# Self-attention scores of a perceiver layer: products of 128 rows by 256 columns, or four row groups of 32 rows by 64 columns over four PSUM banks

## What is computed

```
x = x + cross_attention(layernorm(x), ctx)       # 16 heads of 64, causal, softmax, w_o
x = x + self_attention(layernorm(x))             # 16 heads of 16
x = x + fp4_ffn(layernorm(x))                    # blockwise FP4 rounding of x, h and weights; silu(gate) * up; down
```

```
q, k, v = x @ Wq, x @ Wk, x @ Wv
scores  = q_h @ k_h.T                            # 32 x 32, upper triangle masked to -inf
out_h   = softmax(scores / 16) @ v_h
y       = concat(out_h) @ Wo + bo
```

## Time and profile before

| | us |
|---|---|
| executions | 588.86, 585.85, 585.41 |
| median | 585.85 |
| profiled execution | 588.76 |
| its span, first to last instruction | 586.8 |
| mean granted TensorE clock, share of full speed | 0.968 |

### The profile page before, as it was taken

How to read it: one execution, slowest core, us unless ns; L and a number is a source line. 1 busy time by engine, 2 the same in 40 slices (tenths; PEclk the granted TensorE clock), 3 DMA queues, 4 the chain that set the end, 5 groups by cost and what they waited for, 6 DMA issues and landing times.

```text
span 586.8 us, 18922 instructions
## 1 busy us (share of the span) xinstructions
PE 538.1 (92%) x7926; PEld 429.3 (73%) x7942; DVE 445.3 (76%) x866; ACT 234.2 (40%) x477; POOL 45.6 (8%) x84
## 2 busy tenths in 40 slices
PE   4979999999999999999965989999999999999865
PEld 3768888889888888988743756777777777777543
DVE  3627789888888888888940469988888888888852
ACT  1322233323233332323233456555555555555211
POOL 5000100000000000000020011111111111111100
PEclk9979999999999999999996889999999999999987
DMA  8991210112211012221200000000000000000000
GB/s 255 345 275 72 72 72 25 47 72 72 72 72 72 8 63 72 72 72 73 74 2 4 3 1 2 9 9 9 9 9 9 9 9 9 9 9 10 10 9 19
DMA packets 13801, 31.03 MB, mean 53 GB/s; under 512 B 976, under 2 KB 10704, under 8 KB 11728
## 3 DMA queue, kind: packets, MB, share of 16 engines
q1 hardware_dynamic: 13776, 30.67, 15.7%
HBM read 28.57 MB, written 2.10 MB: 52 GB/s over the span
## 4 chain that ended last, share of the span: by engine, by line
PE 47%; issue 30%; DVE 14%; ACT 4%; POOL 3%; POOLq 0%; DVEq 0%; ACTq 0%
PE bank L378 10%; PE bank L400 10%; PE bank L369 9%; PE bank L425 8%; PE bank L416 3%; ACT x_oT L502 2%; DVE f_xn L1394 2%; POOL f_rstd L1087 2%; DVE f_h L1403 1%; PE bank L1200 1%; PE bank L1178 1%; DVE f_amax_x L1489 1%; DVE f_xn L1528 1%; ACT a_kblocks L1302 1%; PE bank L1154 1%
## 5 line engine op out<-in xcount | busy, mean ns | idle before, releaser
L378 PEld LDWEIGHTS bank<-x_xcT,xwk 128*128 128x128 f32 x512 | 61.3, 197 | 2.8 <-issue 1.1
L378 PE MATMUL bank<-x_xcT,xwk 128*128 128x128 f32 x512 | 61.7, 280 | 1.4 <-ACT x_xcT L485 1.4
L400 PE MATMUL bank<-xwv,x_xcT 128*128 128x512 f32 x128 | 60.8, 618 | 1.0
L369 PE MATMUL bank<-x_xcT,xwq 128*128 128x128 f32 x512 | 59.8, 275 | 0.0
L425 PE MATMUL bank<-xwo,x_oT 128*128 128x256 f32 x256 | 58.0, 380 | 0.8 <-ACT x_oT L502 0.8
L369 PEld LDWEIGHTS bank<-x_xcT,xwq 128*128 128x128 f32 x512 | 58.5, 192 | 0.0
L516 ACT COPY x_k_blocks<-bank 64x512 f32<-64x512 f32 x32 | 18.6, 582 | 87.2 <-PE bank L378 87.0
L425 PEld LDWEIGHTS bank<-xwo,x_oT 128*128 128x128 f32 x256 | 47.5, 190 | 7.2 <-issue 1.4
L1154 PE MATMUL bank<-wdT,f_hqT 128*128 128x256 f32 x192 | 47.6, 400 | 4.3 <-DVEq L1419 2.3
L1302 ACT ACTIVATE a_kblocks<-bank,head_rows 128x256 f32<-128x256 f32 x128 | 48.4, 499 | 0.0
L1178 PE MATMUL bank<-wgT,f_xqT 128*128 128x192 f32 (+1 forms) x128 | 42.3, 475 | 3.7 <-DVE f_out L1360 3.7
(11 more groups left out here) (150 smaller groups left out, 931.4 us busy)
## 6 DMA issues: line engine op xcount, KB each, us to landing
x_ctx_slab<-in_ctx_dram SPq DMA_DIRECT2D x16, 1028.0 KB, 4.7
out_dram<-f_out SPq DMA_DIRECT2D x16, 128.0 KB, 1.7
xall<-in_x_dram SPq DMA_DIRECT2D x1, 1280.0 KB, 16.5
x_first_keys<-in_ctx_dram SPq DMA_DIRECT2D x4, 320.0 KB, 12.5
xwk<-in_L_xattn_w_k_dram SPq DMA_DIRECT2D x1, 1024.0 KB, 5.1
xwq<-in_L_xattn_w_q_dram SPq DMA_DIRECT2D x1, 1024.0 KB, 7.1
xwv<-in_L_xattn_w_v_dram SPq DMA_DIRECT2D x1, 1024.0 KB, 10.2
xwo<-in_L_xattn_w_o_dram SPq DMA_DIRECT2D x1, 1024.0 KB, 12.7
```

The source lines that it names most:

```text
L369: last = nc.tensor.matmul(bank67[:, j // 4, (j % 4) * P:(j % 4 + 1) * P], xwq[:, k, j * P:(j + 1) * P], xcT[:, k, :], start=(k == 0), stop ...
L378: last = nc.tensor.matmul(bank[2 + j // 4][:, (j % 4) * P:(j % 4 + 1) * P], xwk[:, k, j * P:(j + 1) * P], xcT[:, KD + k, :], start=(k == 0 ...
L400: last = nc.tensor.matmul(bank45[:, half, :], xcT[:, KD + k, :], xwv[:, k, half * 512:(half + 1) * 512], start=(k == 0), stop=(k == KD - 1))
```

## The change

Scores are made by 32 small products in place of 8 large ones. The 128 rows of q.T and k.T are eight heads of 16; a row group of 32 rows is two heads. `copy_qk` writes k.T twice, once with the odd and once with the even heads zeroed (`odd_rows`). `scores` multiplies 32 rows by 64 moving columns at `tile_position=(32 r, 32 b)`, row group r into bank 4 + r. The mask is four bf16 products of 128 columns. `odd_rows` is one reduction on VectorE at the end of cross-attention.

Four banks for the scores displace the others: gate goes to banks 2 and 3, transposed `f_xq` and the down product share the free columns of bank 3, q and k go to bank 5, the transposed `f_hq` to banks 4 and 0, v to bank 1 (which `values` and `output` use too), up stays in 6 and 7. With that come new waits on PE: `scores` waits for `f_hidden_ready` and has its two old waits ahead of the mask; `turn_xq` waits for `f_out_ready` and `f_hidden_ready`, no longer for `a_v_ready`; `output` waits for `a_v_ready`; up and `project_qk` wait for `a_shifted`; `project_v` waits for `a_out_ready` in place of `f_hidden_ready`.

```diff
-                a_kb = psb("a_kblocks", [P, KD, BT, HT, SQ])
+                a_kb = psb("a_kblocks", [P, KD, BT, 2, SQ])
...
-                h_bank = (bank[2], bank[0][:, 2 * P:])
-                down_bank = bank45[:, 1, 2 * P:2 * P + D]
+                RG = P // 32
+                HW = KD * 2 * SQ
+                gate_bank, up_bank = bank234567[:, 0:2, :], bank67
+                h_bank = (bank45[:, 0, :], bank[0][:, 2 * P:])
+                qk_bank = bank45[:, 1, :]
+                xq_bank = down_bank = gate_bank[:, 1, 2 * P:2 * P + D]
+                v_bank = bank[1][:, 0:D]
...
-                    def scores(t):
-                        nc.tensor.matmul(bank[2][:], causal_rows[:].rearrange("p b q -> p (b q)"),
-                                         key_copies[:].rearrange("p h k -> p (h k)"), start=True, stop=False)
+                    def scores(t, consumed):
+                        if consumed is not None:
+                            pe.wait_ge(s_f_h, consumed)
                         pe.wait_ge(s_a_kb, t + 1)
                         pe.wait_ge(s_a_qc, t + 1)
+                        for r in range(RG):
+                            nc.tensor.matmul(bank234567[:, 2 + r, 0:HW], causal_rows[:].rearrange("p b q -> p (b q)"),
+                                             key_copies[:, 0:HW // SQ].rearrange("p h k -> p (h k)"),
+                                             start=True, stop=False)
                         for j in range(KD):
-                            for b in range(BT):
-                                last = nc.tensor.matmul(bank[2][b * SQ:(b + 1) * SQ, j * HT * SQ:(j + 1) * HT * SQ],
-                                                        a_qT[:, j, b * SQ:(b + 1) * SQ],
-                                                        a_kb[:, j, b].rearrange("p h k -> p (h k)"),
-                                                        start=False, stop=(j == KD - 1), tile_position=(0, b * SQ))
+                            for r in range(RG):
+                                rows = slice(r * 32, (r + 1) * 32)
+                                for b in range(BT):
+                                    last = nc.tensor.matmul(
+                                        bank234567[b * SQ:(b + 1) * SQ, 2 + r, j * 2 * SQ:(j + 1) * 2 * SQ],
+                                        a_qT[rows, j, b * SQ:(b + 1) * SQ],
+                                        a_kb[rows, j, b].rearrange("p h k -> p (h k)"),
+                                        start=False, stop=(j == KD - 1), tile_position=(r * 32, b * SQ))
                         last.then_inc(s_a_s, 1)
...
-                    def project_v(t, hidden):
-
-                        if hidden is not None:
-                            pe.wait_ge(s_f_h, hidden)
+                    def project_v(t, weighed):
+
+                        if weighed is not None:
+                            pe.wait_ge(s_a_oc, weighed)
                         for k in range(KD):
-                            last = nc.tensor.matmul(bank67[:, 1, D:2 * D], n_xnT[:, k, :], swv[:, k, :],
+                            last = nc.tensor.matmul(v_bank, n_xnT[:, k, :], swv[:, k, :],
                                                     start=(k == 0), stop=(k == KD - 1))
...
                         if attend:
-                            scores(t)
+                            scores(t, t - 2 if down else None)
                         if gate:
-                            turn_xq(t - 2, attend)
+                            turn_xq(t - 2, t - 2 if down else None)
                         if norm:
-                            output(t - 1)
+                            output(t - 1, t + 1 if attend else None)
...
-                        for h in range(HT):
+                        for i in range(2):
                             last = nc.scalar.activation(
-                                a_kb[:, :, :, h, :], bank[3][:, KD * P:].rearrange("p (j b k) -> p j b k", j=KD, b=BT),
-                                ACT.Copy, scale=head_rows[:, h:h + 1])
+                                a_kb[:, :, :, i, :], qk_bank[:, KD * P:].rearrange("p (j b k) -> p j b k", j=KD, b=BT),
+                                ACT.Copy, scale=odd_rows[:, i:i + 1])
```

More of the change, by code:

```diff
@@ L1156, in down_product, with turn_xq, gate_up @@
                         last.then_inc(s_f_d, 1)
[L1158 to L1161, removed]
+                    def turn_xq(t, added):
+                        if not (isinstance(t, int) and t == 0):
                             pe.wait_ge(s_f_h, t)
+                        if added is not None:
+                            pe.wait_ge(s_f_out, added)
                         pe.wait_ge(s_f_xq, t + 1)
                         for k in range(KD):
-                            last = nc.tensor.transpose(bank67[:, 1, k * P:(k + 1) * P], f_xq[:, k * P:(k + 1) * P],
+                            last = nc.tensor.transpose(xq_bank[:, k * P:(k + 1) * P], f_xq[:, k * P:(k + 1) * P],
                                                        ident[:])
                         last.then_inc(s_f_xt, 1)
-                    def gate_up(t, added):
+                    def gate_up(t, added, shifted):
                         pe.wait_ge(s_f_xc, t + 1)
@@ L1174, in gate_up @@
                             pe.wait_ge(s_f_out, added)
-                        for w, dst, done in ((wgT, bank45, s_f_g), (wuT, bank67, s_f_u)):
+                        for w, dst, done in ((wgT, gate_bank, s_f_g), (wuT, up_bank, s_f_u)):
+                            if w is wuT and shifted is not None:
+                                pe.wait_ge(s_a_sh, shifted)
                             for k in range(KD):
@@ L1186, in values @@
                         pe.sem_inc(s_a_begun, 1)
-                        for h in range(H):
+                        for n, h in enumerate(score_heads):
                             for b in range(BT):
@@ L1236, in step @@
                         if gate:
-                            gate_up(t - 2, t - 2 if down else None)
+                            gate_up(t - 2, t - 2 if down else None, t + 1 if attend else None)
                         if down:
@@ L1240, in step @@
                         if project:
-                            project_qk(t + 1)
+                            project_qk(t + 1, t + 1 if attend else None)
                         if attend:
@@ L1246, in step @@
                         if project:
-                            project_v(t + 1, t - 1 if gate else None)
+                            project_v(t + 1, t + 1 if attend else None)
                         if attend:
```

49 lines of the change are left out of this document (31 added, 18 removed).

## The result

| | before | after |
|---|---|---|
| median of 20 executions each | 587.55 us (585.27 to 589.22) | 583.83 us (581.37 to 587.72) |
| ratio of the times, with its 95% interval | | 0.9948 (0.9933 to 0.9964) |
| the profiled execution, its span | 588.76, 586.8 us | 581.37, 579.6 us |
| its mean granted clock | 0.968 | 0.976 |

The account below looks back on a forecast made before the run. PE was taken to bound the loop. Loop -3.1, filling -2.2, clock -1.1, draining +1.0 and one reduction +0.2 sum to -5.2 us: 583.6 for the profiled execution, 580.7 for the median; 8 in 10 from 577.0 to 586.5.

Parts of the forecast that it names:

- DVE's wait: Loop step, ahead of `add_out`, for PE's down product: 1.25 us of room for shortening PE, about 1.0 left afterwards.
- The new waits of the loop: In the loop, waits of v, up, `turn_xq` and the mask: each released early enough, so they cost nothing.
- the rival of columns alone: Scores group: only the four column tiles run side by side, scores +0.02 a step, 585.2 us in all; chance 0.15.
- that of products that hold each other up: Scores group: one product per 55 ns, group 1.90 us, +0.90 and 0.06 a step, 599 in all; chance 0.05.
- One reduction of `odd_rows`: On DVE in cross-attention's last chain: between nothing and 0.42 us, taken as +0.2.
- masks and waits: Loop step: four masks 0.03 us more and PE's queue waits 0.03 more, 0.06 a step.
- draining: Step 17: transposes of `f_xq` now wait for `add_out` and put gate later, +1.0 us, bounds 0.8 and 1.2.
- The scores group: Loop step: 64 records at the pace of `values`, 0.68 us in place of 1.00, saving 0.32 a step.
- The filling: Steps 0 to 2: fewer spreads and shorter scores against v waiting for `a_o`, -2.2 us, allowed -1.2 to -2.8.
- the clock: Half-clock stretch from 320.5 in the filling: -2.2 us if the clock stays full, otherwise 0; even odds, -1.1.
- the prediction's good clock: Filling: the case that the clock stays full, -2.2 us for it beside the filling's -2.2.
- The level: Whole kernel: profiled execution of 588.76 us lies 2.9 above the median of 585.85; the same difference taken off gives 580.7.

Follow-up runs that it names:

- the v experiment: The changed kernel with v in bank 2, waiting for f_h as in the kernel before instead of for `a_o`: 581.34 us, ratio 0.9918 (0.9887 to 0.9948).

## Why the prediction was right or wrong

**What was right.** PE bounded the loop and DVE's wait gave room: it shrank to 1.05, where about 1.0 was forecast. The new waits of the loop cost nothing, each by the cover that was named. Four banks in place of one made DVE's reads no slower (0.68). Both tile directions run side by side: neither the rival of columns alone (group of 1.02) nor that of products that hold each other up (1.90) came. One reduction of `odd_rows` took 0.16 on DVE, against +0.2, and the filling began no later (311.82 against 311.79). The sizes of the other terms were off, some by luck in the right direction: masks and waits cost 0.01 a step and not 0.06, and draining, forecast at +1.0, put gate back by 0.92 but cost 0.3 at the end, because what stood behind gate ran less at half clock.

**The scores group was mis-sized.** The step was "I take the pace of `values`: 64 x 8.4 ns = 0.54, with the 0.14 it is 0.68". It measured 0.79. Halving the columns took only 0.09 off it, halving the records 0.19, so the number of records was the right thing to count; the pace was not constant and the columns added a part. The scores saved 0.21 and not 0.32. With 0.05 less for masks and waits than allowed, the step gained 0.21 (14.91 to 14.70), not 0.26: -2.5 over twelve steps, against -3.1.

**The filling and the clock were taken as two terms and were one.** This is the step that failed most. The prediction had -2.2 for the filling, and for the clock "If it stays full, -2.2; if not, 0. Even odds: **-1.1**", where it asked only about the stretch from 320.5. That stretch does stay full, in every profile, and yet the long executions don't gain what the full clock was to bring. The sum put v's own 0.9 us behind the wait for `a_o` three times. For the kernel at full clock that is about right: v takes 0.97, and the v experiment gives 2.2 for the three. What it didn't ask is how long PE would then idle ahead of v. PE's work ahead of it had become faster and DVE's chain hardly (from the scores of t = 1 to `a_o` 9.0 us, 326.08 to 335.08, where it was 9.2), so the waits are 2.40 and 2.21 us; and in the longer executions the clock falls inside them. From v to gate it is then 6.14 us (336.07 to 342.21) in place of 3.65 (335.08 to 338.73), and from the next v to the transposes of t = 3 17.14 (352.30 to 369.44) in place of 15.67 (348.81 to 364.48): together 4.0 us. Against the long execution of before, the filling up to t = 3 gained 1.1 us in a long one of after (369.44 - 312.69 = 56.75 against 57.86) and 5.2 in a short one (52.66). The short one gains more than the -4.4 of the prediction's good clock, because the second stretch at half clock of before, from 340.9, is gone as well: from the scores of t = 2 to gate it is 2.15 us (336.58 to 338.73) where it was 3.99, and the sum had 0.8 for it. The forecast of -3.3 for both terms stands between two sorts of execution, neither of which has it.

Between like executions, counted from the start of the filling, the sum can be set beside the runs: filling and clock -1.1 in place of -3.3, the loop -2.3 up to t = 14 in place of -2.9, draining +0.3 in place of +1.0, in all -3.1 where these terms had -5.2. That the ratio of the times says -3.1 too is in part luck, since it is taken over a mixture of executions. The rows to ask were there: whoever moves v behind `a_o` can add up DVE's chain from the scores to `a_o` and set it beside q, k and `values` at full clock. PE idled 1.98 us there with v inside the wait, so about 3 were to be expected with v behind it.

**The level was too low.** "I take the same difference off the median" put a sum made against a long execution (588.76 at 0.968) on a median of three, 585.85, that lies by the short ones of before. Over 20 executions the median is 587.55, 1.7 us higher. Applied to 585.85, the measured ratio would give 582.8, 2.1 above the forecast: that is what the sum missed by the ratio. By the two medians of 20 the change gained 3.7 and not 3.1; so of the 3.1 us between 583.83 and the forecast 1.7 are the level and about 1.4 the sum. Why the filling of one kernel meets half clock in some executions only stays open.

One slip changes nothing: by its own terms (0.10 and four tenths of 0.70) the chance of less than 580.0 is 0.38, not 0.37.

## What to carry to other kernels

Where small tiles run side by side, count records as well as columns: 16 products of 128 columns (32 records) took 0.60 us, 32 products of 64 columns (64 records) 0.79. When a result moves to another bank, look for the wait that this brings in the steps without cover, the filling and the draining, and size it against the chain of the other engine, after all the speed-ups ahead of it. And before a sum is put on a median, see whether the profiled execution is one like the median: here the same kernel ran at 581.4 or at 586.9, 4.0 us of it in the filling, where in the one execution the clock fell inside two idle stretches of 2 to 3 us, and 1.4 ahead of it.

## What the runs showed of the hardware

- Sixteen tiles of 32 by 32, in four banks: 32 records start within 0.180 us, at most 8 ns apart; after breaks of 0.086 and 0.055 us they come at about 17 ns a pair and slower at the end. Eight tiles of 64 by 32 with 128 columns run in rounds of about 0.110 us.
- In the filling the stream of small products is now and then cut by 0.4 to 0.6 us with nothing in the profile that would be waited for: 0.42 inside `values` in the rows of the v experiment, 0.58 in its scores at 326.16. At the same places other executions ran through. It was not tried what brings them.
- TensorE's granted clock fell from 2.4 to 1.2 GHz inside waits of 2.73 and 2.22 us in two executions of the changed kernel, and stayed full over waits of 2.40 and 2.21 us at the same places in two others. The kernel with two row groups kept it over 2.73 us there.
- The bf16 masks cost by their columns: one of 512, two of 256 and four of 128 all took 0.38 to 0.39 us, from start to scores 0.31, 0.31 and 0.32.
